# Attention of four graphs and four heads at once, in row and column groups of TensorE, with the maxima added by TensorE

## The reference

```python
def gnn0(x, adj, Wq, bq, Wk, bk, Wv, bv, Wo, bo, gamma, beta):   # 4 heads of 32
    q, k, v = (proj(W, b) for W, b in ((Wq, bq), (Wk, bk), (Wv, bv)))
    attn = jnp.einsum('bhnd,bhmd->bhnm', q, k) * scale
    attn = jax.nn.softmax(jnp.where(adj[:, None] == 0, NEG, attn), axis=-1)
    out = jnp.einsum('bhnm,bhmd->bhnd', attn, v).transpose(0, 2, 1, 3).reshape(Bx, Nx, C)
    out = out @ Wo.T + bo
    return (out - mu) * jax.lax.rsqrt(var + EPS) * gamma + beta
def gnn1(x, adj, Wq, Wk, Wv, Wo, bo): ...                        # the same, 8 heads of 16, no bias, no norm
x = x + gnn0(_layernorm(x), adj, ...);  x = x + ffn0(_layernorm(x), ...)
x = x + gnn1(_layernorm(x), adj, ...);  x = x + ffn1(_layernorm(x), ...)
```

## Time and profile before

| | |
|---|---|
| three runs | 3174.97, 3174.84, 3172.22 us, median 3174.84 |
| the profiled execution | 3169.29 us, span 3167.6 us, mean granted clock 0.98 |
| busy share of the span | TensorE 94%, its weight loads 65%, VectorE 88%, ScalarE 75%, GpSimd 55% |
| first attention | from the start to about 543 us |
| mixture | to about 1054 us |
| second attention | to about 1787 us |
| recurrent stage | to the end |

### The profile page before, as it was taken

The page is one execution under the profiler, slowest core; times in us unless marked ns, Lnnn a source line. Parts: engine busy times, 40 slices in busy tenths (PEclk is TensorE's granted clock), DMA queues, the critical chain, the costliest instruction groups (busy, mean ns, idle before and its releaser), DMA issues. The chain is left out here.

```text
span 3167.6 us, 66950 instructions
## 1 busy us (share of the span) xinstructions
PE 2990.9 (94%) x16831; PEld 2069.3 (65%) x16831; DVE 2796.7 (88%) x8476; ACT 2368.3 (75%) x5280; POOL 1734.2 (55%) x1149
## 2 busy tenths in 40 slices
PE   6989896999999899999999669999999999999999
PEld 4666665888888577777777455555555555555556
DVE  5777776888888788888888779999999999999999
ACT  4666664444444477777777579999999999999994
POOL 2444444333333121212212259999999998888883
PEclk9999998999999999999999779999999999999999
DMA  5000000000000000000000015555555555555555
GB/s 132 18 17 17 17 17 17 1 0 0 0 0 0 22 14 11 13 10 13 10 13 7 3 65 204 192 205 191 202 198 194 207 188 205 194 197 203 190 209 163
DMA packets 132579, 281.63 MB, mean 89 GB/s; under 512 B 11760, under 2 KB 69152, under 8 KB 132512
## 3 DMA queue, kind: packets, MB, share of 16 engines
q1 hardware_dynamic: 115616, 272.44, 24.8%
q10 hardware_dynamic: 16896, 8.39, 0.9%
HBM read 270.49 MB, written 10.29 MB: 89 GB/s over the span
## 5 line engine op out<-in xcount | busy, mean ns | idle before, releaser
L1094 POOL TENSOR_TENSOR d_g<-d_g,d_rb 128x1024 f32<-128x1024 f32 x464 | 1083.9, 2370 | 125.7 <-DMA d_rb<-d_rstd_rows 111.7
L1295 PE MATMUL d_p_y<-d_g,d_w_main 128*128 128x512 f32 x1856 | 952.8, 595 | 0.7 <-POOL d_g L1094 0.7
L1309 PEld LDWEIGHTS d_p_gt<-ident,d_g 128*128 128x128 f32 x3840 | 449.1, 142 | 540.8 <-ACT d_g L1354 399.9
L1173 DVE BATCH_NORM_STATS2 d_stats<-d_p_gt 128x6 f32<-128x256 f32 x1920 | 752.3, 448 | 20.6 <-PE d_p_gt L1309 20.4
L1166 DVE SCALAR_TENSOR_TENSOR d_th<-d_th,d_p_y 128x512 f32<-128x512 f32 x960 | 673.7, 702 | 4.1 <-ACT d_th L1350 4.1
L1354 ACT ACTIVATE d_g<-d_th,d_bias 128x512 f32<-128x512 f32 x928 | 666.9, 719 | 12.9 <-DVE d_th L1166 0.9
L1350 ACT ACTIVATE d_th<-d_p_y,d_bias 128x512 f32<-128x512 f32 x928 | 624.8, 673 | 0.7 <-PE d_p_y L1295 0.7
L1309 PE MATMUL d_p_gt<-ident,d_g 128*128 128x128 f32 x3840 | 590.2, 277 | 0.1
L520 ACT ACTIVATE a_prob<-a_masked,a_neg_max 128x128 f32<-128x128 f32 x1024 | 327.2, 391 | 111.9 <-DVE a_neg_max L335 111.7
L440 PE MATMUL a_p_s<-a_k_heads,a_q_t 128*128 128x512 f32 x768 | 396.4, 598 | 0.5 <-DVE a_k_heads L311 0.5
L457 PEld LDWEIGHTS a_p_pv<-a_v_ones,a_prob_t 128*128 128x128 f32 x3072 | 373.6, 192 | 10.7 <-issue 10.2
(11 more groups left out here) (177 smaller groups left out, 4457.2 us busy)
## 6 DMA issues: line engine op xcount, KB each, us to landing
d_rb<-d_rstd_rows SPq DMA_DIRECT2D x464, 512.0 KB, 5.5
a_adj_in<-in_adj_dram SPq DMA_DIRECT2D x64, 256.0 KB, 2.8
out_dram<-d_out_sb ACTq DMA_DIRECT2D x32, 256.0 KB, 2.7
d_rstd_rows<-d_rstd_row SPq DMA_DIRECT2D x116, 16.0 KB, 1.4
m_w_sb<-in_L_ffn_w_dram SPq DMA_DIRECT2D x2, 512.0 KB
x_sb<-in_x_dram SPq DMA_DIRECT2D x1, 256.0 KB, 2.8
a_w_raw<-in_L_gnn_Wq_dram SPq DMA_DIRECT2D x2, 64.0 KB, 2.2
a_w_raw<-in_L_gnn_Wk_dram SPq DMA_DIRECT2D x2, 64.0 KB, 2.2
```

Of the source, the lines that this page charges most:

```text
L1094: nc.gpsimd.tensor_tensor(g[:, c, :], g[:, c, :], rb[:, buf, :], ALU.mult).then_inc(s_gs, 1)
L1173: ins = nc.vector.bn_stats(stats[:, q % 2, (j * CT + t) // 2].rearrange("p a s -> p (a s)"), p_gt[:, t * P:(t + 2) * P].rearrange("p (a c) ...
L1295: nc.tensor.matmul(p_y[:, c % 2, cols(u)], w_main[:], g[:, c, cols(u)], start=True, stop=True).then_inc(s_y, 1)
L1309: ins = nc.tensor.transpose(p_gt[:, t * P:(t + 1) * P], g[:, c, t * P:(t + 1) * P], ident[:])
```

## The change

Both calls of `graph_attention` are rewritten; the other stages stay. `mask_on_vector` goes, and the mask is added by TensorE in both.

- A unit is now four graphs and four heads: one per quad in the first stage (PARTS = 1), two in the second (PARTS = 2). Its scores fill four banks, `p_s[:, t]` for head t, with no second set. The other four banks (`p_w`, `p_z`, `p_x`, `p_y`) serve transposes, v, q, k, sums, context and projection in turn.
- A product of scores reads the 32 rows of its head in q and k, 128 columns wide; in the second stage 32 rows hold two heads, and the keys are taken twice, with the one head or the other set to zero.
- VectorE takes four maxima of 512 columns, splits the negated maxima into a high and a low bf16 part, TensorE transposes them, VectorE copies, and TensorE adds them to all scores by four 32-row products with a selector. ScalarE then makes one exponential of 512 columns per head, with no bias.
- The sums come from four products with ones in column groups, spread over the 32 rows of each head, and the context comes transposed, in column groups. So VectorE inverts a full 128x512 and multiplies 128x512; no transpose of the context is left.

```diff
-        p_s = pb("p_s", [P, 2, HU, P])
+        p_s = pb("p_s", [P, 4, QG, P])
 # VectorE
+                def maxima(n):
                     dve.wait_ge(s_s, n + 1)
+                    for t in range(4):
+                        last = nc.vector.tensor_reduce(out=row_max[:, t], in_=p_s[:, t], axis=AX.X, op=ALU.max)
+                    last.then_inc(s_max, 1)
                     dve.wait_ge(s_max, n + 1)
+                    wait(dve, s_mt, n)
+                    nc.vector.tensor_scalar(split[:, :, 0:QG], row_max[:], -1.0, None, ALU.mult).then_inc(s_hi, 1)
+                    dve.wait_ge(s_hi, n + 1)
+                    nc.vector.scalar_tensor_tensor(split[:, :, QG:2 * QG], row_max[:], -1.0, split[:, :, 0:QG],
+                                                   ALU.mult, ALU.subtract).then_inc(s_lo, 1)
+                    dve.wait_ge(s_mt, n + 1)
+                    wait(dve, s_sh, n)
+                    nc.vector.tensor_copy(max_t[:], p_z[:, 0:P]).then_inc(s_mtc, 1)
+                def invert_sums(k):
+                    dve.wait_ge(s_den, PARTS * (k + 1))
+                    nc.vector.reciprocal(rden[:], p_y[:]).then_inc(s_rden, 1)
+                def normalise_context(k):
+                    dve.wait_ge(s_pv, PARTS * (k + 1))
+                    dve.wait_ge(s_rden, k + 1)
+                    wait(dve, s_o, k)
+                    nc.vector.tensor_tensor(context_t[:], p_x[:], rden[:], ALU.mult).then_inc(s_ctx, 1)
+                def body(k, par):
+                    if live(k + 2):
+                        stats_x(k + 2)
+                    if live(k):
+                        maxima(PARTS * k)
+                    if live(k - 1):
+                        invert_sums(k - 1)
+                    if normed and live(k - 2):
+                        normalise_projection(k - 2)
+                    if live(k - 1):
+                        normalise_context(k - 1)
+                    if normed and live(k + 2):
+                        normalise_x(k + 2)
+                    if live(k - 1):
+                        take_projection(k - 1)
+                    if normed and live(k - 1):
+                        stats_projection(k - 1)
+                    if PARTS == 2 and live(k):
+                        maxima(PARTS * k + 1)
+                    if not normed and live(k + 2):
+                        normalise_x(k + 2)
 # TensorE
+                def scores(k, par, part):
+                    n = PARTS * k + part
+                    if part == 0:
+                        pe.wait_ge(s_mask, k + 1)
+                    for t in range(4):
+                        wait(pe, s_exp, 4 * (n - 1) + t + 1)
+                        nc.tensor.matmul(p_s[:, t], ident_bf[:], mask[:, par], start=True, stop=False)
                     if part == 0:
                         pe.wait_ge(s_q, k + 1)
                         pe.wait_ge(s_k, k + 1)
+                    for g in range(QG):
+                        for t in range(4):
+                            last = nc.tensor.matmul(p_s[:, t, g], q_t[tile(t), graph(g)], k_t[tile(t), part, graph(g)],
+                                                    start=False, stop=g == QG - 1)
+                    last.then_inc(s_s, 1)
+                def transpose_maxima(n):
+                    pe.wait_ge(s_lo, n + 1)
+                    nc.tensor.matmul(p_z[:, 0:P], split[:], ident_bf[:], start=True, stop=True).then_inc(s_mt, 1)
+                def shift_scores(n):
+                    pe.wait_ge(s_mtc, n + 1)
+                    for t in range(4):
+                        last = nc.tensor.matmul(p_s[:, t], max_t[tile(t), :], selector[tile(t)],
+                                                start=False, stop=True, skip_group_check=True)
+                    last.then_inc(s_sh, 1)
+                def sum_prob(part):
+                    for t in range(4):
+                        last = nc.tensor.matmul(p_y[tile(t), :], ones[:, part, :], prob_t[:, t],
+                                                start=part == 0, stop=part == PARTS - 1)
+                    last.then_inc(s_den, 1)
+                def context_product(par, part):
+                    for g in range(QG):
+                        for t in range(4):
+                            last = nc.tensor.matmul(p_x[tile(t), graph(g)], v_sb[:, par, part, g, tile(t)],
+                                                    prob_t[:, t, g, :], start=part == 0 and g == 0,
+                                                    stop=part == PARTS - 1 and g == QG - 1)
+                    last.then_inc(s_pv, 1)
 # ScalarE
+                def exponentials(n, t):
+                    act.wait_ge(s_sh, n + 1)
+                    wait(act, s_tr, 4 * (n - 1) + t + 1)
+                    nc.scalar.activation(prob[:, t], p_s[:, t], ACT.Exp, scale=EXP_SCALE).then_inc(s_exp, 1)
 # GpSimd, body: the mask now comes right behind rstd, ahead of gamma and beta
                     if live(k + 2):
+                        pool.wait_ge(s_adj[par], ...)
+                        wait(pool, s_s, PARTS * (k + 1))
                         pool.wait_ge(s_var, k + 3)
                         nc.gpsimd.tensor_tensor(rstd[:], var[:], minus_half[:, 0:QG], ALU.pow).then_inc(s_rstd, 1)
+                        nc.gpsimd.tensor_scalar(mask[:, par], adj_in[:, par], 0.0, MASKED, masked_op,
+                                                ALU.mult).then_inc(s_mask, 1)
```

More of the change, by code:

```diff
@@ L423, in _ @@
[L423 to L425 removed]
+                    pe.wait_ge(s_prep, 10)
+                    for t, bank in enumerate((p_z[:, 0:P], p_s[:, 0, 0], p_s[:, 1, 0], p_y[:, 0:P])):
+                        last = nc.tensor.matmul(bank, bv_bc[tile(t), :], w_o[tile(t), :], start=True, stop=True)
@@ new lines, in scores, with transpose_prob @@
+                    for g in range(QG):
[3 more added lines that the diff above has]
+                    last.then_inc(s_s, 1)
+                def transpose_prob(n, t, bank):
+                    pe.wait_ge(s_exp, 4 * n + t + 1)
+                    for g in range(QG):
+                        last = nc.tensor.transpose(bank[:, graph(g)], prob[:, t, g, :], ident[:])
+                    last.then_inc(s_tr, 1)
@@ new lines, in transpose_x @@
+                def transpose_x(k):
+                    pe.wait_ge(s_xn, k + 1)
+                    for g in range(QG):
+                        last = nc.tensor.transpose(p_w[:, graph(g)], xn[:, g, :], ident[:])
+                    last.then_inc(s_xt, 1)
+                def transpose_maxima(n):
[7 more added lines that the diff above has]
+                    last.then_inc(s_sh, 1)
@@ new lines, in take_v @@
+                def take_v(k, par):
+                    act.wait_ge(s_vmm, k + 1)
+                    wait(act, s_pv, PARTS * (k - 1))
+                    if PARTS == 1:
+                        nc.scalar.copy(v_sb[:, par, 0], by_graph(p_z)).then_inc(s_v, 1)
+                        return
+                    for part in range(2):
+                        dst = v_sb[:, par, part].rearrange("p g c -> p (g c)")
+                        last = nc.scalar.copy(by_head(dst)[:, :, part], by_head(p_z[:])[:, :, part])
+                    last.then_inc(s_v, 1)
@@ new lines, in take_xn, with body @@
+                def take_xn(k):
+                    act.wait_ge(s_xt, k + 1)
+                    wait(act, s_vmm, k)
+                    wait(act, s_kmm, k)
+                    nc.scalar.copy(xn_t[:], p_w[:]).then_inc(s_xtc, 1)
+                def body(k, par):
+                    for part in range(PARTS):
+                        n = PARTS * k + part
+                        before = live(k) if part else live(k - 1)
+                        even, odd = PARTS == 1 or part == 0, PARTS == 1 or part == 1
+                        if before:
+                            take_prob(n - 1, 0)
+                            take_prob(n - 1, 1)
+                            take_prob(n - 1, 2)
+                        if odd and live(k + 1):
+                            take_q(k + 1)
+                        if PARTS == 2 and even and live(k):
+                            take_v(k, par)
+                        if before:
+                            take_prob(n - 1, 3)
+                        if odd and live(k + 1):
+                            take_k(k + 1)
+                        if live(k):
+                            for t in range(4):
+                                exponentials(n, t)
+                        if PARTS == 1 and live(k + 1):
+                            take_v(k + 1, 1 - par)
+                        ahead = k + 2 if PARTS == 1 else k + 1
+                        if even and live(ahead):
+                            take_xn(ahead)
```

472 lines of the change are left out of this document (194 added, 278 removed).

## The result

The changed kernel takes 3299.0 us (3298.2 to 3300.7), the kernel before 3174.9 (four runs of each); the ratio is 1.039, with a 95% interval from 1.038 to 1.041. The forecast was 3268 us, slower. Its profiled execution has a span of 3296.5 us, 128.9 more than before. The mixture starts at 672.5 us where it started at 543.8, so all of the loss lies in the first attention stage; the second is 2 us shorter than before, and the other stages keep their length within 2 us.

What follows compares the result with a forecast made beforehand. TensorE bound both attention stages; after the change, a row of waits through VectorE's reciprocal would. First stage +2.2 and second +0.7 us per quad, times 32, add 93 to 3169: 3262, plus 6 for the median, 3268 us; range 3010 to 3420.

Steps and rivals of the forecast that it cites:

- Split at 3.5, with half a wait for GpSimd's mask: First stage, VectorE: maxima split by 3.5 us after the scores end, 0.4 of it half the loss to GpSimd's mask.
- Sums and reciprocal, from 4.85 to 8.55: First stage: after TensorE's sums, VectorE's 512-wide reciprocal starts at 4.85 us and takes 3.7, priced by element.
- x normalised at 12.1, with 1.8 us: First stage, VectorE: four operations on x, 1.1 us alone, meet GpSimd's three products and end at 12.1 us.
- (c): First stage: x's four operations wait for each of GpSimd's three, 2.5 us more per quad, 3350 us; chance 0.10.
- From x to the next scores 4.3, and 1.6 for the clock: First stage, TensorE: x's transposes through the next scores, 12.1 to 16.4 us, plus 1.6 per quad for the clock dip.
- First stage 18.0: First attention stage: 16.4 us per quad plus 1.6 for the clock makes 18.0, against 15.8 before.
- Second stage 22.9 with a dip of 1.0: Second attention stage: 21.9 us per quad plus 1.0 for the clock makes 22.9, against 22.2 before.
- (a): VectorE's wide reciprocal costs one cycle per element, 0.7 us: quads of 13.4 and 19.8 us, 3021 us; chance 0.20.
- The point of decision of 2.2 us for the reciprocal: Both stages: (a) decides with the reciprocal below 2.2 us, each microsecond of it being 64 us of time.
- (b): Both attention stages: the reciprocal is slow but TensorE's clock holds, +10 us, 3185 us; chance 0.15.
- (d): TensorE's tiles take turns: sums and scores 2.6 us more each on the row, +500 us, near 3700; chance 0.04.
- (e): TensorE stays at half clock through both attention stages, some +400 us, near 3660 us; chance 0.05.

Runs made afterwards that it cites:

- The run with GpSimd later: The changed kernel with GpSimd's three operations waiting until VectorE has written the normalised x: 3200.8 us, ratio 1.009 to the kernel before.
- The filled run: The changed kernel with TensorE's first-stage pause ahead of the transposes of x filled with 22 products of 128x512: 3237.7 us, ratio 1.020 to the kernel before.
- the run that has one: The changed kernel with the attention reciprocal replaced by a 0.69 us VectorE instruction that writes 1.0: 3097.0 us, ratio 0.976 to the kernel before.
- the order run: The changed kernel with the score loops exchanged, all four graphs of one row group one behind the other: 3423.0 us, ratio 1.078 to the kernel before.

## Why the prediction was right, and where it was not

The sign, the stage and the mechanism were right: 3268 forecast, 3299 measured, in the range. Step by step, in the quad shown above, from the end of the scores (VectorE sees it 0.2 later, so 307.39):

- *Maxima 2.7*: 2.7. *Split at 3.5, with half a wait for GpSimd's mask*: at 3.1; the small operation took 0.17 us while the mask ran (308.80 to 310.74). The wait that I read out of the earlier trace rows is one for products, not for this mask.
- *Sums and reciprocal, from 4.85 to 8.55*: from 4.6 to 8.0. The reciprocal, the term that decided, measures 3.36 us (0.34 below the value taken, far from 0.7), or (3.36 - 0.16) / 512 = 6.2 ns for each element. To take it by element, from an excess of 0.02 us over four, was right. By the walkthrough in the Trainium skill (VectorE: DVE Perf Modes, walkthrough of the 8-slice pipeline) I had an estimate of 4.3 us; the trace doesn't bear that out, it is a fifth less.
- *Context at 10.3*: at 9.5.
- *x normalised at 12.1, with 1.8 us*: at 13.1, with 3.7. This is the first term that was mis-sized. I let VectorE wait for one of GpSimd's three products, as in the earlier trace rows, and gave the longer wait to rival (c). The trace shows a first slice beside a product and a last that ends with another: the timing between the two engines is set by VectorE's own order, so it repeats in every quad. The run with GpSimd later puts the cost at 2.2 us at full clock. (c) was right for part of the time, though its 2.5 us came on top of a wait that I had counted.
- *From x to the next scores 4.3, and 1.6 for the clock*: from the start of x's transposes at 300.30 to 307.39, 7.1 us. The filled run takes 4.4 for the same at full clock, so the 4.3 was right and the clock's part is 2.7 in this quad; in the mean it is 2.2. I took it from one dip that began inside a unit, of which scores, transposes and context products were stretched; behind a pause of 6.2 us it is x's transposes, the projection, two banks of probabilities and the masks, up to six microseconds of work. This is the second mis-sized term.
- *First stage 18.0*: -0.8 up to the context, +1.8 for x and +1.2 behind it make 20.2, the period of this quad; the mean is 19.8.
- *Second stage 22.9 with a dip of 1.0*: 21.9. Without any dip my row had 21.9; the quads without one take 21.2, and about every second one has a dip, of 1.7 (22.9). The row was 0.7 too long, the reciprocal and the split again, and the mean dip is 0.7, not 1.0. Against before the stage gained 2 us in all, where I had +0.7 a period.

The errors had opposite signs: +1.8 us a period in the first stage, -1.0 in the second, which is why the sum is off by 31 us only and not by 58. That closeness is luck; what was right is the row and the reciprocal as the term that decides.

Of the rivals, (a) gave 3021 us for a cheap reciprocal; the run that has one gave 3097. Its second stage was well sized (19.1 us against 19.8), but for the first it assumed 13.4 and the run has 16.4, for a pause of 3.6 us and the wait for GpSimd remain, and with them a clock of 0.90. The point of decision of 2.2 us for the reciprocal was drawn from 64 us for each microsecond; the run shows 202 / 2.67 = 76. (b) is refuted by the clock row. (d) is refuted by the order run: with the groups one behind the other it is another kernel, 124 us slower. (Its sum was off as well: 500 us on top of the forecast are 3768, not 3700.) (e) didn't come about: the clock came back in each quad.

What I did not see is that the work for which TensorE waits was there, behind the longest operation in VectorE's queue: x normalised for two quads ahead needs nothing from the reciprocal, and to move it is worth 5.3 us a period.

## What to carry to other kernels

A change that frees the bound engine is worth what the next row allows: write that row down with each engine's queue order, and price an operation that grows from 4 to 512 elements by its excess per element, since that one term can take the whole gain. Then look at what stands behind the new long operation without needing it; here one moved block on VectorE and one on TensorE turned +3.9% into -3.2%. A long pause of TensorE can cost more than its length: here the work behind 6.2 us of it ran at half clock and took 2.2 us more in the mean, and a filler showed how much.

## What the hardware showed beyond expectation

- GpSimd's products of 128x512 hold up VectorE's scalar operations from SBUF to SBUF, small ones too: x normalised 3.71 us against 1.10, a 128x4 operation 0.92 and 1.10 against 0.17. The batch statistics beside them keep their 0.76 us, what reads PSUM its 0.69 (L325 at 310.08 above), and the mask did not hold up the split. The Trainium skill (SBUF — State Buffer, Who interferes with whom) describes a port pair that the two engines share, which certain forms of VectorE's operations need and where the loser is blocked for a whole instruction. The trace agrees as far as the lengths tell: two of the four slices of x last 1.42 and 1.28 us beside products of 1.26, and one between them 0.33. That the mask doesn't block, no run here explains.
- Behind a pause of TensorE of 6.2 us the clock was 0.50 for 2.8 to 6.1 us of work; with pauses of 2.5 us once per 22 us about every second quad had a dip, worth 1.7 us; with the pause broken into 1.13 and 0.32 us none had.
- Score products of different row groups start within 0.02 us (four from 306.345 to 306.365 us in the changed kernel), the records of one row group 0.11 us apart, and 16 products spread over four groups take 1.17 us against 2.81 in turn, so the order in which they are issued is worth 1.6 us a unit.
